# Statistics of six tiles by ScalarE, and the first gate products in four groups of 32 output partitions

## What is computed

```python
x = x + attn(layernorm(x), ...)             # projects to 128 channels, 4 layers, projects back
x = x + xattn(layernorm(x), ctx_4096, ...)  # the pooling stage
x = x + ffn(layernorm(x), gate_w, expert_w) # 8 experts, each token goes to its top 2

def xattn(x, ctx, ...):                     # per batch and channel, over the 256 tokens
    mask = 1 at the 154 largest of ctx, else 0
    crucial, rest = mask * x, (1 - mask) * x
    a1 = sigmoid(relu(norm(conv([max, mean] of crucial))))   # max and mean over tokens
    a2 = sigmoid(relu(norm(conv([max, mean] of rest))))      # norm over all batches and channels
    return crucial * a1 + rest * a2

def ffn(x, gate_w, expert_w):
    logits = x @ gate_w                     # 1024 -> 8, float32, decides the experts
    p = softmax(top 2 of logits)
    return sum of p * (x @ expert_w[e]) over the two experts
```

## Time and profile before

| | us |
|---|---|
| median of three timed runs | 1079.43 (1075.89 to 1080.05) |
| profiled execution | 1075.65 |
| its span, first to last instruction | 1073.8 |
| TensorE busy | 987.2 (92%) |
| VectorE busy | 554.4 (52%) |
| ScalarE busy | 383.4 (36%) |
| GpSimd busy | 453.3 (42%) |
| expert products, L2106 | 509.8 |
| mean granted clock of TensorE | 0.965 |

### The profile page before, as it was taken

The page is one execution under the profiler, slowest core; times in us unless marked ns, Lnnn a source line. Parts: engine busy times, 40 slices in busy tenths (PEclk is TensorE's granted clock), DMA queues, the critical chain, the costliest instruction groups (busy, mean ns, idle before and its releaser), DMA issues. The chain is left out here.

```text
span 1073.8 us, 13204 instructions
## 1 busy us (share of the span) xinstructions
PE 987.2 (92%) x3508; PEld 518.4 (48%) x3515; DVE 554.4 (52%) x1547; ACT 383.4 (36%) x1032; POOL 453.3 (42%) x567
## 2 busy tenths in 40 slices
PE   5888999898999797999379999999999999999995
PEld 5786665555555453345234444444444444444442
DVE  5648899999998799879942111111111111111111
ACT  2436888797884287678400000000000000000000
POOL 3756755665541011068054444333334333334441
PEclk9989999899999899999689999999999999999998
DMA  7511020200003210026858463737346373473332
GB/s 296 176 60 41 11 89 11 88 1 2 1 1 148 109 58 1 1 82 257 315 208 255 137 171 76 230 70 230 73 119 186 78 232 78 84 228 78 78 78 40
DMA packets 38462, 120.25 MB, mean 112 GB/s; under 512 B 6220, under 2 KB 9351, under 8 KB 38408
## 3 DMA queue, kind: packets, MB, share of 16 engines
q1 hardware_dynamic: 25592, 79.77, 20.3%
q0 software_dynamic: 12816, 39.86, 16.9%
HBM read 82.91 MB, written 36.70 MB: 111 GB/s over the span
## 5 line engine op out<-in xcount | busy, mean ns | idle before, releaser
L2106 PE MATMUL bank<-T,X 128*128 x1184 | 509.8, 593 | 1.4 <-DVEq L2156 1.4
L2106 PEld LDWEIGHTS bank<-T,X 128*128 128x128 f32 x1184 | 225.5, 191 | 285.8 <-issue 285.8
L2154 DVE TENSOR_SCALAR X<-bank,col_p 128x512 f32<-128x512 f32 x37 | 27.8, 751 | 388.1 <-PE bank L2106 385.7
L2127 ACT ACTIVATE X<-bank,col_p 128x512 f32<-128x512 f32 x37 | 25.4, 687 | 494.0 <-PE bank L2106 469.7
L2066 POOL DMA_INDIRECT out_dram<-X,col_d x37 | 60.0, 1622 | 260.9 <-DVE X L2154 244.7
L2057 POOL DMA_INDIRECT X<-x_nrm,col_s x152 | 145.5, 957 | 50.9 <-issue 46.2
L490 POOL TENSOR_TENSOR rs<-ve,neg_half 128x4 f32<-128x4 f32 x36 | 43.8, 1217 | 100.6 <-DVE ve L979 100.1
L849 ACT ACTIVATE M<-X,T 128x256 bf16<-128x256 f32 x152 | 75.1, 502 | 0.0
L665 PE MATMUL bank<-nat,T 128*128 128x512 f32 x128 | 64.5, 621 | 4.1 <-DVE nat L985 1.5
L1502 DVE STREAM_TRANSPOSE X<-X 128x1024 f32<-128x1024 f32 x39 | 48.4, 1240 | 33.0 <-DMA X<-x_nrm,col_s 27.9
L673 PE MATMUL bank<-X,T 128*128 128x512 f32 x128 | 57.9, 595 | 0.0
(11 more groups left out here) (341 smaller groups left out, 1425.2 us busy)
## 6 DMA issues: line engine op xcount, KB each, us to landing
T<-in_L_ffn_expert_w_dram SPq DMA_DIRECT2D x8, 4096.0 KB, 17.6
out_dram<-X SPq DMA_DIRECT2D x17, 512.0 KB
M<-in_x_dram SPq DMA_DIRECT2D x16, 512.0 KB, 7.3
X<-in_x_dram SPq DMA_DIRECT2D x16, 512.0 KB, 5.5
x_nrm<-H SPq DMA_DIRECT2D x16, 512.0 KB, 3.8
T<-in_ctx_dram SPq DMA_DIRECT2D x9, 512.0 KB, 3.5
X<-x_nrm,col_s POOLq DMA_INDIRECT x152
X<-in_ctx_dram SPq DMA_DIRECT2D x4, 512.0 KB, 6.9
```

Of the source, the lines that this page charges most:

```text
L2106: mm = nc.tensor.matmul(bank[2 * u + n][:, :], xgt[u][:, k, :], Tf[:, ds(odd * D + (k * N + n * BANK), BANK)], start=(k == 0), stop=(k == ...
```

## The change

Two things change, and some names move to make room.

1. The row tiles 5, 7, 9, 11, 13 and 15 (`SQUARED`) no longer go through `ln_stats`. ScalarE's `rows` of such a tile keeps the sum of each half as it copies. In turn `t - 2` (`AHEAD`) VectorE makes the mean of the two sums (`squared_mean`), ScalarE squares both halves less the mean with a sum (`squared_tile`), and GpSimd adds the two, scales them and adds the epsilon (`squared_var`) ahead of `ln_pow`.
2. `gate` is widened from 8 to 32 columns per k, with zeros behind the 8 weights. The first gate products of k = 0 to 7 write partitions 32j to 32j + 31 of the bank with j = k mod 4, so that a bank holds four partial sums. `first_sums` copies 128 partitions instead of 8, and `first_turned` is a matmul with `sum_e`, a 128 x 8 matrix of ones and zeros that adds the four, instead of a transpose.

```diff
+GROUPS = 4
+GROUP_E = 128 // GROUPS
...
-        gate = sb("gate", [P, KD, E])
+        gate = sb("gate", [P, KD, GROUP_E])
+        SQUARED = [t for t in range(FIRST_TILES, NT) if t % 2 == 1]
+        AHEAD = 2
         def counted(m, t):
-            return m * NT + t + 1 - (sum(on_scalar(*divmod(i, CT)) for i in range(t + 1)) if m == 1 else 0)
+            if m == 0:
+                return t + 1 - sum(i in SQUARED for i in range(t + 1))
+            return NT - len(SQUARED) + t + 1 - sum(on_scalar(*divmod(i, CT)) for i in range(t + 1))
+        def sum_at(t, k):
+            n = 4 * (SQUARED.index(t) % 4) + k
+            return back_of(0, n)
         def rows(act, t):
             for n in range(2):
                 hold(act, o2_mm, 2 * t + n + 1)
-                nc.scalar.copy(X[:, t, n * BANK:(n + 1) * BANK], bank[2 + 2 * (t % 2) + n][:, :]).then_inc(x1_done, 1)
+                from_bank = bank[2 + 2 * (t % 2) + n][:, :]
+                if t in SQUARED:
+                    nc.scalar.activation(X[:, t, n * BANK:(n + 1) * BANK], from_bank, ACT.Copy, accum_out=sum_at(t, n)).then_inc(x1_done, 1)
+                else:
+                    nc.scalar.copy(X[:, t, n * BANK:(n + 1) * BANK], from_bank).then_inc(x1_done, 1)
...
+                sp.wait_ge(gate_clear, 1)
-                sp.dma_start(gate[:, :, :], gate_w.rearrange("(k p) e -> p k e", p=P)).then_inc(ld_gate, 16)
+                sp.dma_start(gate[:, :, 0:E], gate_w.rearrange("(k p) e -> p k e", p=P)).then_inc(ld_gate, 16)
...
+                g.memset(gate[:, :, :], 0.0).then_inc(gate_clear, 1)
                 g.memset(ident[:, :], 0.0).then_inc(const_ready, 1)
...
+        def of_group(sums, k):
+            j = k % GROUPS
+            return sums[j * GROUP_E:(j + 1) * GROUP_E, :]
             for k in range(first, last):
-                mm = nc.tensor.matmul(bank[P1_SUMS[c]][0:E, :], gate[:, k, :], T[:, k, c * GROUP:(c + 1) * GROUP], start=(k == 0), stop=(k == KD - 1))
+                mm = nc.tensor.matmul(of_group(bank[P1_SUMS[c]], k), gate[:, k, :], T[:, k, c * GROUP:(c + 1) * GROUP], start=(k < GROUPS), stop=(k >= KD - GROUPS))
...
+                def squared_var(t):
+                    n = SQUARED.index(t)
+                    var = ve_all(0)[:, t:t + 1]
+                    pool.wait_ge(sq_sum, n + 1)
+                    nc.gpsimd.tensor_tensor(var, sum_at(t, 2), sum_at(t, 3), ALU.add).then_inc(sq_var, 1)
+                    pool.wait_ge(sq_var, 2 * n + 1)
+                    nc.gpsimd.tensor_scalar(var, var, 1.0 / D, EPS, ALU.mult, ALU.add).then_inc(sq_var, 1)
+                    pool.wait_ge(sq_var, 2 * n + 2)
                 for t in range(CT, NT):
+                    if t in SQUARED:
+                        squared_var(t)
                     ln_pow(pool, 0, t)
...
-                        mm = nc.tensor.transpose(bank[P1_BANK][:, t * E:(t + 1) * E], by_expert[c % 2][:, u * P:(u + 1) * P], ident[0:E, 0:E])
+                        mm = nc.tensor.matmul(bank[P1_BANK][:, t * E:(t + 1) * E], by_expert[c % 2][:, u * P:(u + 1) * P], sum_e[:, :], start=True, stop=True)
...
+                def squared_tile(t):
+                    hold(act, sq_mean, SQUARED.index(t) + 1)
+                    hold(act, cr_sum, min(max(t - AHEAD - LAG - 1, 0), UNITS))
+                    for n in range(2):
+                        ins = a.activation(wide_junk[n], X[:, t, n * BANK:(n + 1) * BANK], ACT.Square, scale=-1.0, bias=mean_of(0, t),
+                                           accum_out=sum_at(t, 2 + n))
+                    ins.then_inc(sq_sum, 1)
                 for t in range(NT + LAG + 2):
...
+                    if t + AHEAD in SQUARED:
+                        squared_tile(t + AHEAD)
                     if 0 <= t - LAG - 1 < UNITS:
                         sums(t - LAG - 1)
...
+                def squared_mean(t):
+                    hold(dve, x1_done, 2 * t + 2)
+                    v.tensor_scalar(mean_of(0, t), sum_at(t, 0), sum_at(t, 1), 1.0 / D, ALU.add, ALU.mult).then_inc(sq_mean, 1)
                 for t in range(NT + LAG + 1):
-                    if CT <= t < NT:
+                    if t + AHEAD in SQUARED:
+                        squared_mean(t + AHEAD)
+                    if CT <= t < NT and t not in SQUARED:
                         hold(dve, x1_done, 2 * t + 2)
                         ln_stats(dve, 0, t)
...
-                link(v.tensor_reduce(g_part, gate[:, :, :].rearrange("p k e -> p e k"), AX.X, ALU.add))
+                v.tensor_reduce(sum_e[:, :], ident[:, :].rearrange("p (j e) -> p e j", j=GROUPS)[:, 0:E, :], AX.X, ALU.add)
+                link(v.tensor_reduce(g_part, gate[:, :, 0:E].rearrange("p k e -> p e k"), AX.X, ALU.add))
...
-                    v.tensor_copy(by_expert[c % 2], bank[P1_SUMS[c]][0:E, :]).then_inc(p1_cp, 1)
+                    v.tensor_copy(by_expert[c % 2], bank[P1_SUMS[c]][:, :]).then_inc(p1_cp, 1)
```

More of the change, by code:

```diff
@@ L149, in decoder_kernel @@
         ld_gate = sem("ld_gate")
+        gate_clear = sem("gate_clear")
         const_ready = sem("const_ready")
@@ L295, in decoder_kernel @@
         e_stat, e_mean, e_ve, e_rt, e_bc, e_bcs, e_h = (sem(n) for n in ("e_stat", "e_mean", "e_ve", "e_rt", "e_bc", "e_bcs", "e_h"))
-        wo_tp, wo_ev, wo_set, bo_mm = (sem(n) for n in ("wo_tp", "wo_ev", "wo_set", "bo_mm"))
+        wo_ev, wo_set = (sem(n) for n in ("wo_ev", "wo_set"))
         TABLE_STEPS = 1 + 11 * (NT // 2)
@@ L898, in _ @@
                     if s == -4:
-                        act.wait_ge(wo_tp, 1)
+                        act.wait_ge(set_pe, 4)
                         for n in range(2):
@@ L1223, in _ @@
                     if s == -3:
-                        dve.wait_ge(bo_mm, 1)
+                        dve.wait_ge(set_pe, 5)
                         dve.wait_ge(ld_bout, 16)
@@ L1308, in decoder_kernel @@
         pooled = ewide[:, 0:4 * KD * B].rearrange("p (m i k b) -> p m i k b", m=2, i=2, k=KD)
-        logits = sb("logits", [P, NT, E])
+        logits = center[:, :].rearrange("p (t e) -> p t e", e=E)
         totals = logits[:, :, :].rearrange("p t e -> p (t e)")[:, 0:KD * B].rearrange("p (k b) -> p k b", k=KD)
@@ L1313, in decoder_kernel @@
         junk = [spill[:, k, :] for k in range(2)] + [late[:, JUNK + k * S // 2:JUNK + (k + 1) * S // 2].bitcast(BF16) for k in range(2)]
+        wide_junk = [spill[:, :, :].rearrange("p k s -> p (k s)"), late[:, JUNK:JUNK + S].bitcast(BF16)]
         x1_tp, t_set = sem("x1_tp"), sem("t_set")
+        sq_mean, sq_sum, sq_var = (sem(n) for n in ("sq_mean", "sq_sum", "sq_var"))
         cr_mul, cr_sum, re_max, av_set = (sem(n) for n in ("cr_mul", "cr_sum", "re_max", "av_set"))
@@ L1359, in decoder_kernel @@
         g_part = in_late(E)
+        sum_e = in_late(E)
         known = in_late(NT, E)
@@ L1458, in decoder_kernel @@
         P1 = N // GROUP
-        by_expert = [fin[0:E, u, :] for u in range(2)]
+        by_expert = [fin[:, u, :] for u in range(2)]
         def expert_src(e):
@@ L1490, in decoder_kernel @@
         col_s = [sb(f"col_s{u}", [P, QK], U32) for u in range(IN_FLIGHT)]
-        col_d = [sb(f"col_d{u}", [P, 1], U32) for u in range(IN_FLIGHT)]
-        col_p = [sb(f"col_p{u}", [P, 1]) for u in range(IN_FLIGHT)]
+        col_d = [mv[:, u, 0:1].bitcast(U32) for u in range(IN_FLIGHT)]
+        col_p = [ve[:, u, 0:1] for u in range(IN_FLIGHT)]
         xg_in = [sem(f"xg_in{u}") for u in range(IN_FLIGHT)]
@@ L1640, in second_part @@
                     for k in range(KD):
-                        mm = nc.tensor.matmul(bank[P2_SUMS[b % 2]][0:E, 0:S], gate[:, k, :], T[:, k, b * S:(b + 1) * S], start=(k == 0), stop=(k == KD - 1))
+                        mm = nc.tensor.matmul(bank[P2_SUMS[b % 2]][0:E, 0:S], gate[:, k, 0:E], T[:, k, b * S:(b + 1) * S], start=(k == 0), stop=(k == KD - 1))
                     mm.then_inc(p1_mm, 1)
@@ L1647, in second_turned @@
                         t = CT * b + h
-                        mm = nc.tensor.transpose(bank[P2_BANK][:, t * E:(t + 1) * E], by_expert[b % 2][:, h * P:(h + 1) * P], ident[0:E, 0:E])
+                        mm = nc.tensor.transpose(bank[P2_BANK][:, t * E:(t + 1) * E], by_expert[b % 2][0:E, h * P:(h + 1) * P], ident[0:E, 0:E])
                     mm.then_inc(l_mm, 1)
@@ L1710, in sums @@
                     hold(act, cr_mul, n + 1)
+                    before = sum(t - AHEAD <= n + LAG + 1 for t in SQUARED)
+                    if before > 0:
+                        hold(act, sq_sum, before)
                     if n > 0:
@@ L1908, in second_sums @@
                     hold(dve, p1_mm, P1 + b + 1)
-                    v.tensor_copy(by_expert[b % 2][:, 0:S], bank[P2_SUMS[b % 2]][0:E, 0:S]).then_inc(p1_cp, 1)
+                    v.tensor_copy(by_expert[b % 2][0:E, 0:S], bank[P2_SUMS[b % 2]][0:E, 0:S]).then_inc(p1_cp, 1)
                 for k in range(KU):
```

10 lines of the change are left out of this document (5 added, 5 removed).

## The result

The changed kernel took 1082.76 us in the median of seven runs (1079.36 to 1087.06), the kernel before 1079.43 (1075.89 to 1080.30) in seven beside it: a ratio of 1.0051, 95% interval 1.0031 to 1.0071. The forecast was no change within 0.5%, and the ratio lies just above that bound. The forecast of 1079.7 us was 3.1 us under the median; the range of 1073 to 1085 holds it. The profiled execution took 1081.07 us, its span 1079.2.

What follows compares the result with a forecast made beforehand. It took VectorE to bound the pooling loop, with TensorE 13% behind, and only the expert products' start to move. Terms -3.0 + 2.6 + 0.2 + 0.5 = +0.3 us gave 1079.7 us at the median, range 1073 to 1085.

Steps and rivals of the forecast that it cites:

- The gain of 10.8 us: VectorE in the pooling loop: 12.3 us of statistics removed, 1.5 us of means added, if no new waits came.
- The loop's -3.0: Pooling loop: `normed(12)` comes as before, then tiles 13 and 15 save 4.1 us and pay 1.1.
- the first wait: Turn 3 of the loop: VectorE stands still 4.2 us until row tile 5 is out of its bank.
- the four waits behind it: VectorE's later waits in the loop up to `normed(12)`, forecast as about 3 x 0.84 + 0.6 us.
- ScalarE's pair: ScalarE's work per two loop tiles: 9.46 us, 10.1 with waits, ending last so VectorE waits 0.8 us in each.
- The tail behind tile 12: Loop's end: tiles 13 and 15 save 4.1 us and pay one mean and one wait, 1.1: -3.0 us.
- The clock, +2.6: Normalisation chain behind the loop: emptier TensorE starts it at clock 0.50, costing 2.1 + 0.5 us; bounds 0 and 4.1.
- One sign of being wrong: TensorE's granted clock standing at 1.00 at 450 us, where the forecast expected 0.50 as the chain starts.
- Overlap of the products: Grouped first gate products on TensorE take 0.55 of their time; gain on the path 0 to 0.1 us.
- Behind the loop: +0.7 forecast: Between chain and `second_part(0)`: +0.2 us for the reduction making `sum_e`, +0.5 for the last `first_turned` call.
- The slow rival: Gates: TensorE idle over 3 us ahead of `back(0)`, so `back(0)` and second parts start at 0.50; 1086 to 1088 us, chance 0.07.
- The ScalarE term: Pooling loop, with ScalarE's pair ending last: -3.0 us at the loop's end.

Runs made afterwards that it cites:

- e4: Changed kernel with `sums` ahead of the squares in ScalarE's turn; median 1079.10 us, ratio 1.0017 to the kernel before, loop 83.80 us.
- e3: Changed kernel plus 30 dense matmuls, results unused, on TensorE ahead of the normalisation chain; median 1080.49 us, ratio 1.0022 to the kernel before.
- e8: Kernel before, with the 24 gate passes ahead of the normalisation chain moved behind it; one profiled run, 1088.73 us, chain 9.28 us.
- e1: Changed kernel with no squared tiles, so grouped gate products alone; median 1085.38 us, ratio 1.0061 to the kernel before.
- e7: e4 with e3's 30 dense matmuls and 16 more ahead of `back(0)`; median 1077.48 us, ratio 0.9992 to the kernel before.
- e10: e7 with 8 more dense matmuls ahead of `back(1)`; median 1073.49 us, ratio 0.9966 to the kernel before.

## Why the prediction was right, and where it was not

- **No change in sum, and a loop limited by ScalarE: right in kind.** VectorE waits for rows as forecast: 4.63 us in the first turn for 4.2, then 1.1 to 1.7 for 0.84 in a pair. The gain of 10.8 us went into waits of 10.8 us. That the time lies in the range is owed to the range's width too: the sum said +0.3 us where the stages show +4.5, and two of its terms were well off.
- **The loop's -3.0: the term that failed, it was +0.3.** The step that failed is that `normed(12)` would come at the same time as before. It came 59.9 us after the loop's start for 57.2 before, 2.7 later. Of these, 0.4 stood in the forecast's own working, which saves 8.2 and pays 8.6 us, and was taken for nothing in the sum; 0.4 is the first wait (4.63 for 4.2); and 1.9 are the four waits behind it, 5.1 us for the 3.1 allowed. Those follow from ScalarE's pair, 10.63 us where 10.1 was taken: its work is 9.85 us for 9.46 (the two squares 1.5 for 1.3, the four row copies 2.3 for 2.1), its waits 0.78 for 0.65. One pair, with waits of 1.42 us, took 11.27. I had laid out how long ScalarE's instructions last, and not what `sums` waits for on its own engine. The tail behind tile 12 gave 2.4 of its 3.0 us. e4 removes the waits, has 9.85 us in a pair and -3.1 us for the loop; that this is the forecast's -3.0 is chance, since the forecast had the waits in it.
- **The clock, +2.6: right in mechanism, too small.** It was +3.8, near the upper bound of 4.1. The chain's first matmuls took 4.31 us for 2.28, as forecast. Too small was the price of the first six dense matmuls, which held up the sum's matmul by 1.3 us (2.56 for 1.29) where 0.5 was taken; and the second six, left out of the sum, took 2.08 us for the 1.46 of such a six, since the clock came back only in 464 to 465 us. One sign of being wrong was named as a clock of 1.00 at 450 us. In 450 to 451 us it was 1.00, but all marks lie some 5 us later than forecast, the loop's end at 455.2 for 449.7; at the chain's start, which the sign meant, it was 0.50. e3 and e8 show the cause from both sides.
- **Overlap of the products: 0.55 of the time forecast, 0.27 measured** (0.12 for 0.44 us). I let two neighbours overlap; the rows show a pass costing about a quarter. On the path it only moved TensorE's end forward, as the forecast said, so it changed how cold TensorE got and nothing else. The Trainium skill (TensorE: Matmul & The Clock Gate, Part 3) has 2.38x for three column tiles. No run here has three; four sets of 32 gave 7.03 / 1.92 = 3.7x, on float32 products.
- **Behind the loop: +0.7 forecast, +1.0 measured,** of which `sum_e` is nothing (its reduction is there, 0.21 us at 467.54, yet from the start of L1908 to that of L1972 VectorE took 2.69 us, as from L1849 to L1912 before) and the last turn of the sums the rest. The forecast put one call of `first_turned` on the path at +0.5. Two stand there, of groups 2 and 3 (16 passes at 480.19), at some 0.6 us more each: from the first of their copies on VectorE to `second_part(0)` it is 2.63 us (479.44 to 482.07) for 1.67 (473.11 to 474.78).
- **The slow rival (TensorE cold again in the gates):** in the changed kernel `back(0)` was cold, 3.54 us, and nobody felt it; `second_part(0)` was not. In e1, e3 and e7 it was, for 1.4 to 1.9 us and not the 6 to 8 that I gave that rival. Its condition, TensorE idle for over 3 us ahead of `back(0)`, was met and did make `back(0)` cold, but it wasn't what decided on `second_part(0)`: the passes ended 3.9 us ahead of `back(0)` in the changed kernel as well as in e3.
- **A reading of the earlier trace rows.** TensorE's wait of 0.59 us for `normed` wasn't only at tile 12: the trace before has it at tiles 10 and 11 too (0.59 and 0.58 us), so TensorE had caught up with VectorE from tile 10 on. No term hung on it.
- **The sum.** The ScalarE term and the clock term erred the same way, 3.3 and 1.2 us, with 0.3 more behind the loop and 0.6 us back in gates and routing: 4.2 us, with the forecast's own +0.3 the 4.5 of the stages. I had let such errors cancel; these two added up.

What stays open: what decides whether `second_part(0)` runs cold. e3's rows before it are those of the changed kernel with a warmer start, and yet it is e3 that falls.

## What to carry to other kernels

When work moves to an engine that has air, lay out that engine's queue with every hold on it, also those between its own instructions; the order of two helpers on ScalarE was worth 3.5 us here, more than the price of any instruction. Shortening work that nobody waits for isn't free on TensorE: what stood ahead of a chain of small matmuls kept the clock up, and without it the chain went from 5.5 to 9.3 us. Measure the parts of a change alone: here one cost 0.6%, and the other, in a better order, gained 0.5%.

## What the runs showed of the hardware

- Four sets of 32 output partitions run side by side: a float32 pass of 128x512 takes 0.12 us (16 in 1.92) where it took 0.44 in a single set of 8. The order of issue, two passes to a set and then the next, was no obstacle.
- The granted clock fell to 0.50 at 481 us in e3 although TensorE's busy share was 0.59 to 1.00 in the three windows before; what ran there were 128-column transposes and products of 8 columns. In e10, with 8 dense matmuls of 512 columns between them and less idle time, the same products ran at 1.00; in the changed kernel, with neither, they did so too. What decides is open.
- A square of 128x512 with its sum on ScalarE occupies 0.72 us, a copy of that size out of a bank 0.47, with its sum 0.57.
